# First expert stage of a four-layer attention and mixture-of-experts kernel: one region per expert over both turns, 71 tiles instead of 78, all its rows written inside the block before it

## The chip, the core and the metric

One Trainium2 chip, one core of it. The metric is device time in microseconds (us), the median of several executions. All times are from the profile of one execution, or from the timed runs where that is said. The engines are called PE (TensorE), DVE (VectorE), ACT (ScalarE), POOL or GpSimd, and SP (SyncE, which here only issues DMAs).

## The reference, cut to what matters

`x` is [32, 128, 128]: 4096 rows of 128 values. Four layers, each an attention and an expert stage, each added to x:

```python
x = x + _L0_xattn_ref(ctx_1024, _layernorm(x), ...)     # two hops of softmax attention over ctx
x = x + _L0_ffn_ref(_layernorm(x), router_w, w1, b1, w2, b2)
x = x + _L1_xattn_ref(_layernorm(x), ctx_1024, ...)     # linear attention, 16 heads of 8
x = x + _L1_ffn_ref(_layernorm(x), ...)                 # top 2 of 8, capacity 256 rows an expert
x = x + _L2_xattn_ref(ctx_1024, _layernorm(x), ...)     # 16 heads of 64 over ctx and x
x = x + _L2_ffn_ref(_layernorm(x), ...)                 # top 2 of 8, silu gate
x = x + _L3_xattn_ref(_layernorm(x), ctx_1024, ...)     # one head
x = x + _L3_ffn_ref(_layernorm(x), ...)                 # top 1 of 8
```

The first expert stage, which the change is named for, is, for each row,

```python
router_logits = x @ router_w.T
topk_values, topk_indices = top_k(router_logits, 2)      # of 8 experts
topk_weights = softmax(topk_values)
h1 = gelu(x @ w1[e].T + b1[e])                           # 128 -> 512
expert_outputs = h1 @ w2[e].T + b2[e]                    # 512 -> 128
mixed_output = sum over the two chosen e of topk_weights * expert_outputs
```

## The kernel before, in words

The kernel is a row of blocks. A block is one program for each engine; at its end every engine waits for all the others, GpSimd's queue ends with a drain, and then the next block begins. In order: a small load block, `attention_0`, `experts(0)`, `attention_1`, `route(1)`, `experts(1)`, `attention_2`, `experts(2)`, `attention_3`, `experts(3)` and the final sum and store. Below they are also called the first attention, the first expert stage, and so on.

**Attentions 0, 1 and 3** work in two turns (TURNS) of four interleaved streams (W) of four 128-row tiles (G), so 16 tiles (N) a turn. Each turn ends with a layer norm, the router logits, and the top two of them. In attention 0 the engines then count how many rows go to each expert (two matmuls with a triangle and with ones, L808), DVE copies the counts (`counted`, L896) and works out for every row its place in a table in DRAM (`places`, L902, which ends with `first_positions`). GpSimd then writes the rows there: `spread_row` (L657) is one indirect DMA of 128 rows of 129 words, of which the last word is the number of the output row. Each tile goes out twice, for the first and the second choice; between the two GpSimd rewrites the last word (`second_choice`, L664, which ends with a GpSimd drain). Both turns make 64 such DMAs. SP writes a tile of padding at the end of each expert's rows (L716 to L721), for each turn.

**The table of the first expert stage** (`xturn`) has a region for each expert and turn, each padded to whole tiles, so the stage has 2 x 39 = 78 tiles (TILES_FIRST) to work through. The order of the tiles and the expert of each come from `tile_tables` (L629), called once a turn at the end of attention 0. Because the regions are kept apart by turn, the stage can start when the first turn's rows are there: of the second turn's 32 DMAs, 8 are issued inside attention 0 (L764), 7 at the start of the stage (LAST_ROWS_AHEAD), and the other 17 one by one behind its scatters (`late_spread`, L670, and L1319).

**An expert stage** is a pipeline over tiles of 128 rows. SP loads the tile of rows into one of eight slots (`load_tile`, L1258); PE turns it; DVE copies the turned tile and the 516 columns of the expert's first weights (L1414, L1416); PE makes the hidden rows (L1345); ACT applies gelu (L1379); PE makes the output (L1357); DVE adds the bias (L1408) and GpSimd scatters the 128 output rows to their places in DRAM (L1318). SP's first loads are issued after the stage has begun, in stage 0 after it has waited for padding and rows. In stages 0 and 3 ACT issues a 512 KB load of the second bias (`load_b2`, L1252), and DVE waits for it before its first copy. Stages 2 and 3 are the same with 71 and 39 tiles; stage 2 has a silu gate and no bias. Stage 1 gathers its rows by another path.

**Weights.** Stage 1's weights (3 MB) are loaded by SP inside stage 0, behind the first eight tiles (L1272). Stage 3's (4 MB) are loaded by ACT, first thing in stage 2 (L1387).

**Attention 2** has 128 units (32 tiles by four quarters of the heads) in a software pipeline, so its head runs before the first unit can start: SP brings four tiles' pairs of expert rows (512 KB, `stage`, L1836); GpSimd multiplies and adds them into x (`add_pairs`, L1914), DVE takes mean and variance and makes the reciprocal root by a bit trick and three Newton steps (`seed`, `refine`, L2158 to L2167), GpSimd scales the rows (`scale_rows`), PE turns them and ACT keeps them. The context rows take a path of their own (`norm_context`). At the end of attentions 2 and 3 GpSimd waits until all spread rows have landed (L1993, L2394), and the block ends.

## Time and profile before

| | |
|---|---|
| median of 3 runs | 1893.69 us (1891.07 to 1894.52) |
| the profiled execution | 1896.3 us; its span 1894.4 us |
| busy in the span | PE 79%, weight loads 71%, DVE 62%, ACT 44%, POOL 41% |
| mean granted TensorE clock | 0.865 of full speed |
| DMA | 84.67 MB, mean 45 GB/s |

Stages on the profile's clock, read from SP's timeline (the first DMA that SP issues in a block comes less than 1 us after the block has begun): attention 0 to 199.6; expert stage 0 from there to 404.6; attention 1, route and stage 1 to 670.5; attention 2 to 1467.2; stage 2 to 1617.2; attention 3 to 1781.7; stage 3 to 1875.9; final sum to 1894.4.

How to read it: the busy shares are means over stages with different limits, and an engine that is idle in one stage says nothing of the next. The chain of waits that the profile prints reaches back only to the last block's start, so for a change in the earlier blocks the timelines at the block borders have to be read instead.

### The profile page before, as it was taken

What the parts mean: (1) busy time and instruction counts of PE and PEld (TensorE: products, weight loads), DVE (VectorE), ACT (ScalarE), POOL (GpSimd) and SP (SyncE); (2) the same over time, 40 slices, a digit from 0 to 9 for tenths busy, and PEclk for the clock granted to TensorE, in tenths of its full rate; (3) what the DMA queues carried; (4) which work ended last, traced back from release to release, by engine and by line L of the source; (5) the groups of instructions that cost most, each with busy time, mean ns of one, the idle gap of its engine ahead of it and who ended that gap; (6) DMA issues with size and microseconds to landing.
All of it is one profiled execution on the core that took longest, in us unless ns stands there. A gap on an engine that the chain in (4) does not pass through costs nothing. (4 is left out here: it accounts for less than half of the span.)

```text
span 1894.4 us, 37385 instructions
## 1 busy us (share of the span) xinstructions
PE 1492.4 (79%) x10501; PEld 1343.0 (71%) x10502; DVE 1165.8 (62%) x3709; ACT 834.1 (44%) x2565; POOL 776.9 (41%) x769
## 2 busy tenths in 40 slices
PE   6575589966577639999999999999993798446294
PEld 4454579954466639999999999999993787235294
DVE  4536234438867337787877777777775455575244
ACT  3342335531222226666666666666661232323152
POOL 2034454420000635454747575656454355012442
PEclk8776789987766769999999999999997899766697
DMA  9311422230011120000000000000001522200223
GB/s 231 13 29 41 136 58 64 64 107 0 1 45 45 41 93 13 1 12 1 24 1 22 1 21 11 11 3 8 4 10 35 149 72 66 90 7 16 64 65 115
DMA packets 96551, 84.67 MB, mean 45 GB/s; under 512 B 17444, under 2 KB 83207, under 8 KB 96327
## 3 DMA queue, kind: packets, MB, share of 16 engines
q1 hardware_dynamic: 75048, 49.50, 10.3%
q0 software_dynamic: 12160, 25.01, 3.9%
q10 hardware_dynamic: 9248, 9.05, 1.6%
q8 instruction: 41, 0.67, 0.1%
q14 instruction: 54, 0.44, 0.1%
HBM read 52.92 MB, written 32.70 MB: 45 GB/s over the span
## 5 line engine op out<-in xcount | busy, mean ns | idle before, releaser
L1973 POOL TENSOR_TENSOR paired_rows<-paired_rows,rinv 128x1024 f32<-128x1024 f32 x128 | 242.5, 1895 | 284.9 <-DVE rinv L2258 281.7
L2137 ACT ACTIVATE paired_rows<-psum_banks,neg_max 128x256 f32<-128x256 f32 x512 | 237.8, 490 | 0.2
L2249 DVE TENSOR_TENSOR probs_turned_lo<-psum_banks,probs_turned_hi 128x512 fp32r<-128x512 f32 x256 | 175.6, 686 | 97.6 <-ACT probs_turned_hi L2119 84.3
L2023 PE MATMUL psum_banks<-y_turned_parts,queries_hi 128*128 128x256 f32 x1024 | 200.7, 294 | 3.0 <-DVEq L1874 3.0
L2058 PE MATMUL psum_banks<-probs_turned_hi,y_rows 128*128 128x512 f32 x512 | 192.2, 416 | 0.4 <-issue 0.4
L2119 ACT CAST probs_turned_hi<-psum_banks 128x512 fp32r<-128x512 f32 x256 | 151.1, 590 | 57.2 <-PE psum_banks L2007 54.8
L2023 PEld LDWEIGHTS psum_banks<-y_turned_parts,queries_hi 128*128 128x128 f32 x1024 | 159.1, 192 | 3.5 <-issue 3.5
L2007 PE MATMUL psum_banks<-ident,paired_rows 128*128 128x128 f32 x1024 | 155.0, 274 | 7.4 <-DVEq L1874 4.4
L2263 DVE TENSOR_REDUCE neg_max<-psum_banks 128x4 f32<-128x1024 f32 x128 | 155.9, 1218 | 7.1 <-PE psum_banks L2023 3.5
L2119 ACT CAST queries_hi<-psum_banks 128x512 fp32r<-128x512 f32 x128 | 75.1, 587 | 172.0 <-PE psum_banks L2046 167.4
L2023 PE MATMUL psum_banks<-y_turned_parts,queries_lo 128*128 128x256 f32 x512 | 145.3, 284 | 0.0
L2070 PEld LDWEIGHTS psum_banks<-expert_w_a,paired_rows 128*128 128x128 f32 x1024 | 133.9, 191 | 11.8 <-DVE paired_rows L2273 1.0
L2046 PE MATMUL psum_banks<-expert_w_b,expert_w_a 128*128 (+1 forms) x1024 | 138.3, 278 | 3.3 <-ACT tail_turned L2109 1.8
L2070 PE MATMUL psum_banks<-expert_w_a,paired_rows 128*128 128x128 f32 x1024 | 134.9, 275 | 0.8 <-issue 0.8
L1379 ACT ACTIVATE hidden<-psum_banks,tile_w 128x128 f32<-128x128 f32 x312 | 89.6, 369 | 102.5 <-PE psum_banks L1345 77.1
L2046 PEld LDWEIGHTS psum_banks<-expert_w_b,expert_w_a 128*128 128x128 f32 x1024 | 125.8, 193 | 7.3 <-ACT tail_turned L2109 3.2
L2007 PEld LDWEIGHTS psum_banks<-ident,paired_rows 128*128 128x128 f32 x1024 | 119.5, 142 | 10.3 <-DVEq L1874 5.1
L2249 DVE TENSOR_TENSOR queries_lo<-psum_banks,queries_hi 128x512 fp32r<-128x512 f32 x128 | 88.4, 691 | 43.1 <-ACT queries_hi L2119 34.6
L2137 ACT ACTIVATION_READ_ACCUMULATOR paired_rows<-psum_banks,neg_max 128x1 f32 x512 | 113.2, 221 | 0.0
L1318 POOL DMA_INDIRECT expert_rows<-expert_rows_sb,tile_rows x78 | 76.8, 985 | 80.7 <-DVE expert_rows_sb L1408 77.1
L2058 PEld LDWEIGHTS psum_banks<-probs_turned_hi,y_rows 128*128 128x128 f32 x512 | 96.3, 188 | 17.7 <-issue 0.5
L658 POOL DMA_INDIRECT rows_by_expert_and_turn<-paired_rows,top_experts x64 | 62.0, 969 | 111.5 <-ACT u_turned___ L841 60.6
(699 smaller groups left out, 3440.5 us busy)
## 6 DMA issues: line engine op xcount, KB each, us to landing
paired_rows<-expert_rows SPq DMA_DIRECT2D x16, 512.0 KB, 6.0
tile_rows<-rows_by_expert_and_turn SPq DMA_DIRECT2D x78, 64.5 KB
tile_rows__<-rows_by_expert SPq DMA_DIRECT2D x71, 64.5 KB
staged_pairs<-expert_rows SPq DMA_DIRECT2D x8, 512.0 KB
tile_rows___<-rows_by_expert SPq DMA_DIRECT2D x39, 64.5 KB
x_rows<-in_x_dram SPq DMA_DIRECT2D x8, 256.0 KB, 5.4
expert_w_b<-in_L_ffn_w_dram SPq DMA_DIRECT2D x1, 2048.0 KB
normed_rows_dram<-paired_rows SPq DMA_DIRECT2D x1, 2048.0 KB, 8.8
```

Of the source, the lines that this page charges most:

```text
L1318: pool.indirect_dma_start(ys, bass.IndirectOffsetOnAxis(ap=to, axis=0), yo[:, i % SLOTS, :], None).then_inc(expert_out[i % SLOTS].sem, 16)
L1379: ins = act.activation(hidT[:, s % 2, c * P:(c + 1) * P], hidden_bank(s, c // 2)[:, c % 2 * P:(c % 2 + 1) * P], ACT.Gelu, bias=w1[:, s % 4 ...
L1973: ins = pool.tensor_tensor(probs[:, p, :, :], probs[:, p, :, :], rinv[:, p, :].unsqueeze(2).to_broadcast([P, 4, 256]), ALU.mult)
L2007: ins = pe.transpose(bank[T_BANK][:, h * P:(h + 1) * P], probs[:, par, h, c * P:(c + 1) * P], ident[:, :])
L2023: ins = pe.matmul(bank[S_BANKS[par] + h // 2][:, (h % 2) * 256:(h % 2 + 1) * 256], queries[q][:, h, :], yparts[:, 2 * s2 + y, :], start=(k ...
L2046: ins = pe.matmul(bank[Q_BANK][:, h * P:(h + 1) * P], wqk[:, 4 * u3 + h, :], flat(KVT[:, bass.ds(b3, 1), P:2 * P]), start=True, stop=True)
L2058: ins = pe.matmul(bank[Z_BANK][:, :], yrows[:, 2 * s1 + y, k * P:(k + 1) * P], probsT[p][:, (u + 1) % 2, k, :], start=(k == 0 and n == 0), ...
L2070: ins = pe.matmul(bank[Y_BANK][:, 0:P], mixed[:, par, h, :], wvo[:, 4 * u0 + h, :], start=(u0 == 0 and h == 0), stop=(u0 == 3 and h == 3), ...
L2119: ins = act.copy(dst, bank[bank_][:, :])
L2137: ins = act.activation(probs[:, par, h, :], bank[S_BANKS[par] + h // 2][:, (h % 2) * 256:(h % 2 + 1) * 256], ACT.Exp, bias=nmax[:, par, h: ...
L2249: ins = dve.tensor_tensor(lo, bank[bank_][:, :], hi.bitcast(F32), ALU.subtract)
L2263: ins = dve.tensor_reduce(nmax[:, par, :], ps[:, S_BANKS[par]:S_BANKS[par] + 2, :].rearrange("p r (h k) -> p (r h) k", k=256), AX.X, ALU.m ...
```

## The change

The table `xfirst` takes the place of `xturn`: one region per expert over both turns, so the first expert stage has 71 tiles. The second turn's counts begin where the first's ended (`begin` from `ends0`), `tile_tables` is called once, and padding is written once (8 DMAs instead of 16). All 64 row DMAs are issued inside attention 0. `second_choice` no longer drains GpSimd; it waits on a semaphore of its own copy. At the end of attention 0 SP waits for all rows and loads the first two tiles (AHEAD) of the next stage before the block ends; attentions 2 and 3 do the same, and there GpSimd's wait for the rows moves to SP. The slots for tiles (`tile_rows`) are therefore one buffer for the whole kernel. Stage 1's weights are loaded in attention 1, stage 3's in attention 3, both by SP behind the pairs. In attention 0 PE waits for DVE's copy of the counts only before stream 0's keys in the next turn, and ACT's small exponential comes after the weight copies. In attention 2's head DVE does the first four tiles' sums, ACT makes the roots by logarithm and exponential, and DVE scales the rows; GpSimd only scales the context rows. Parts of the diff that rename or move buffers are left out below.

```diff
-TILES_TURN = (B * P + E * (P - 1)) // P
-TILES_FIRST = 2 * TILES_TURN
-TURN_TILES = E * TURN_REGION // P + E - 1
...
-            for i in range(TURNS):
-                at = (i * TURN_TILES + E * TURN_REGION // P) * P
-                mine = 2 * E + i * SPARE_TILES
-                sp.dma_start(as_tiles(xturn[at:at + SPARE_TILES * P, :]), pad_tiles[:, mine:mine + SPARE_TILES, :]).then_inc(pads_stored.sem, 16)
+            sp.dma_start(as_tiles(xfirst[E * REGION:, :]), pad_tiles[:, 2 * E:2 * E + SPARE_TILES, :]).then_inc(pads_stored.sem, 16)
...
+        def rows_are_here(sp):
+            for c in first_rows_spread:
+                sp.wait_ge(c.sem, TURNS * 16 * N)
+
+        def place_first_pads(sp):
+            sp.wait_ge(first_ends.sem, 1)
+            for e in range(E):
+                at_ = sp.value_load(first_pad_at[0:1, e:e + 1], min_val=0, max_val=E * REGION - P)
+                sp.dma_start(xfirst[bass.ds(at_, P), :], pads_dram[e * P:(e + 1) * P, :]).then_inc(first_pads.sem, 16)
+
+        def load_rows(sp, layer, j, s, free):
+            rows = xfirst if layer == 0 else xb
+            at = sp.value_load(tile_base[0:1, bass.ds(j, 1)], min_val=0, max_val=E * REGION // P + SPARE_TILES - 1)
+            if not isinstance(j, int) or j >= SLOTS:
+                free()
+            src = rows.rearrange("(t p) d -> t p d", p=P)[bass.ds(at, 1), :, :].rearrange("a p d -> (a p) d")
+            sp.dma_start(tile_rows[:, s, :], src).then_inc(tile_loaded[s].sem, 16)
+
+        def load_first_tiles(sp, layer):
+            sp.wait_ge(tables_made.sem, tables_made.value + 1)
+            for j in range(AHEAD):
+                load_rows(sp, layer, j, j, None)
...
-            pool.tensor_copy(ROWS.bitcast(U32)[:, at, P], odd_number[:, at])
-            pool.drain()
-
-        def late_spread(pool):
-
-            for t in range(N // 2, N):
-                spread_row(pool, TURNS - 1, 0, t)
-                yield
-            for half in range(2):
-                second_choice(pool, TURNS - 1, half)
-                for t in range(half * N // 2, (half + 1) * N // 2):
-                    spread_row(pool, TURNS - 1, 1, t)
-                    yield
...
-                    for i in range(TURNS):
-                        sp.wait_ge(first_ends.sem, i + 1)
-                        for e in range(E):
-                            at_ = sp.value_load(first_pad_at[0:1, i * E + e:i * E + e + 1], min_val=0, max_val=2 * TURN_TILES * P - P)
-                            n = (i * E + e) * P
-                            sp.dma_start(xturn[bass.ds(at_, P), :], pads_dram[n:n + P, :]).then_inc(first_pads.sem, 16)
+                    place_first_pads(sp)
+                    sp.wait_ge(first_pads.sem, 16 * E)
+                    rows_are_here(sp)
+                    load_first_tiles(sp, 0)
...
-                    spread_first(pool, 1, 0, 0)
+                    for half in range(2):
+                        spread_first(pool, 1, 0, half)
+                    for half in range(2):
+                        second_choice(pool, 1, half)
+                        spread_first(pool, 1, 1, half)
...
+                        if w == 0:
+                            pe.wait_ge(first_places_read.sem, i + 1)
...
-                        dve.tensor_copy(begin[:, 0, :], region[:, i, :])
+                        dve.tensor_copy(begin[:, 0, :], ends0[:, i - 1, :] if i else region[:, :])
...
-                    def turn_is_here(i):
-                        for c in first_rows_spread:
-                            sp.wait_ge(c.sem, (i + 1) * 16 * N)
-                    if layer == 0:
-                        sp.wait_ge(first_pads.sem, 16 * TURNS * E)
-                        turn_is_here(0)
+                        load_rows(sp, layer, j, s, lambda: slot_is_free(sp, j, s))
                     if kept:
-                        for j in range(SLOTS):
+                        for j in range(AHEAD, SLOTS):
                             load_tile(j, j)
-                    if layer == 0:
-                        load_expert_weights(sp, layer + 1)
...
-                        loops = [(1, n_tiles // SLOTS)]
-                        if layer == 0:
-                            loops = [(1, TILES_TURN // SLOTS), (TILES_TURN // SLOTS + 1, n_tiles // SLOTS)]
-                        for turn, (begin_, end_) in enumerate(loops):
-                            if turn:
-                                for j in range(loops[0][1] * SLOTS, begin_ * SLOTS):
-                                    if j == TILES_TURN:
-                                        turn_is_here(1)
-                                    load_tile(j, j % SLOTS)
-                            with sp.Fori(begin_, end_) as q:
-                                for u in range(SLOTS):
-                                    load_tile(q * SLOTS + u, u)
+                        with sp.Fori(1, n_tiles // SLOTS) as q:
+                            for u in range(SLOTS):
+                                load_tile(q * SLOTS + u, u)
...
-                    late = late_spread(pool) if layer == 0 else iter(())
-                    for _ in range(LAST_ROWS_AHEAD):
-                        next(late, None)
...
-                    if layer == 2:
-                        load_expert_weights(act, layer + 1)
...
                     load_pairs(sp, layer_before)
+                    load_expert_weights(sp, 1)
...
                     place_pads(sp, range(E // 2), 0)
                     sp.wait_ge(pads_placed.sem, 16 * E)
+                    sp.wait_ge(rows_spread.sem, 16 * 2 * G * NG)
+                    load_first_tiles(sp, 2)
...
-                    for c in range(10):
-                        norm_part(0, c)
+                    norm_context(0)
...
+                def roots(act, own, which):
+                    act.wait_ge(spread_known.sem, spread_known.value + which)
+                    act.activation(row_work[:, 2, own], row_work[:, 0, own], ACT.Ln, scale=-2.0)
+                    act.drain()
+                    act.activation(row_rstd[:, own], row_work[:, 2, own], ACT.Exp, scale=-0.5).then_inc(roots_made.sem, 1)
...
-                    dve.wait_ge(pairs_combined.sem, 1)
+                    dve.wait_ge(pairs_staged.sem, 16)
+                    for k in range(2):
+                        for j in range(G):
+                            xt = x_tile(0)(j)
+                            ins = dve.scalar_tensor_tensor(xt, staged[:, j, k, :], WT[:, k, j:j + 1], xt, ALU.mult, ALU.add)
+                        ch.link()
+                    dve.sem_inc(pairs_combined.sem, 1)
                     row_stats(dve, ch, 0, 0)
                     aggregate(dve, ch, [0])
-                    seed(dve, ch)
-                    refine(dve, ch, 3)
-                    keep_scales(dve, ch, 0, None)
+                    dve.tensor_scalar(row_work[:, 0, :], row_mv[:, :, 1], -0.5 * (1.0 + EPS), -0.5 * EPS * EPS, ALU.mult, ALU.add).then_inc(spread_known.sem, 1)
+                    dve.wait_ge(roots_made.sem, roots_made.value + 1)
+                    refine(dve, ch, 1)
+                    for j in range(G):
+                        ins = dve.tensor_scalar(latents[:, j, :], x_tile(0)(j), row_mv[:, j, 0:1], row_rstd[:, j:j + 1], ALU.subtract, ALU.mult)
+                    ins.then_inc(latents_normed.sem, 1)
+                    dve.sem_inc(scales_made.sem, 1)
                     all_steps(lambda eng, i, c: dve_step(eng, ch, i, c))(dve)
...
                     load_pairs(sp, layer_before)
+                    load_expert_weights(sp, 3)
                     place_pads(sp, range(E // 2), 1)
                     sp.wait_ge(pads_placed.sem, 2 * 16 * E)
+                    sp.wait_ge(rows_spread.sem, 16 * (2 * B + B))
+                    load_first_tiles(sp, 3)
 
```

## Rows read from the trace of the kernel before

**Rows 1.** Stretches of the first and last expert stages; columns in the first line.

```profile
core 0: us, PE busy (x) PEld busy (x) DVE busy (x) ACT busy (x) POOL busy (x), PEclk, DMA share, GB/s
...
212.00:224.00 12.00, 8.91 (x74) 8.26 (x72) 4.04 (x13) 4.94 (x18) 4.58 (x7) 1.00 0.94 299
...
224.00:271.00 47.00, 32.87 (x213) 31.20 (x213) 11.12 (x36) 14.10 (x49) 28.01 (x30) 0.82 0.24 63
...
271.00:387.00 116.00, 115.55 (x937) 109.82 (x938) 53.10 (x166) 63.29 (x223) 54.61 (x56) 0.99 0.21 62
...
1792.00:1870.00 78.00, 76.73 (x632) 72.40 (x630) 35.36 (x110) 42.32 (x148) 37.86 (x39) 1.00 0.20 58
```

**Rows 2.** GpSimd in the first attention: start us, us, instruction, idle before and releaser.

```profile
145.26 0.21 POOL L667 COPY paired_rows<-odd_number 128x8 uint32<-128x8 uint32 x1
...
148.01 0.98 POOL L658 DMA_INDIRECT rows_by_expert_and_turn<-paired_rows,top_experts  x1 [2.55 <-issue]
...
182.65 0.96 POOL L658 DMA_INDIRECT rows_by_expert_and_turn<-paired_rows,top_experts  x1 [12.52 <-DVE top_experts L913]
...
200.34 0.96 POOL L658 DMA_INDIRECT rows_by_expert_and_turn<-paired_rows,top_experts  x1 [7.59 <-POOLq L682]
```

**Rows 3.** GpSimd in the first expert stage, same columns.

```profile
211.24 0.96 POOL L1318 DMA_INDIRECT expert_rows<-expert_rows_sb,tile_rows  x1 [2.36 <-DVE expert_rows_sb L1408]
...
274.07 0.96 POOL L1318 DMA_INDIRECT expert_rows<-expert_rows_sb,tile_rows  x1 [1.77 <-DVE expert_rows_sb L1408]
...
395.55 0.96 POOL L1318 DMA_INDIRECT expert_rows<-expert_rows_sb,tile_rows  x1 [0.30 <-DVE expert_rows_sb L1408]
```

**Rows 4.** GpSimd's queue, drains that end four blocks, by source line; ns min/median/max.

```profile
L682 POOLq DRAIN  x1: 9023/9023/9023, 185.8 to 185.8; - x1
...
L1781 POOLq DRAIN  x1: 1354/1354/1354, 1465.8 to 1465.8; - x1
...
L2352 POOLq DRAIN  x1: 2656/2656/2656, 1778.8 to 1778.8; - x1
...
L1196 POOLq DRAIN  x1: 5845/5845/5845, 1611.2 to 1611.2; - x1
```

**Rows 5.** Timelines: first and last expert stage begin (ACT, SP), last stage's scatters (GpSimd).

```profile
200.47 11.49 SPq L1264 DMA_DIRECT2D tile_rows<-rows_by_expert_and_turn  x8
...
1781.76 0.36 ACTq L1252 DMA_DIRECT2D expert_b___<-in_L_ffn_b_dram  x1
...
1792.20 0.98 POOL L1318 DMA_INDIRECT expert_rows<-expert_rows_sb___,tile_rows___  x1 [14.87 <-DVE expert_rows_sb___ L1408]
...
1869.87 0.97 POOL L1318 DMA_INDIRECT expert_rows<-expert_rows_sb___,tile_rows___  x1 [0.31 <-DVE expert_rows_sb___ L1408]
```

**Rows 6.** Timelines (GpSimd, DVE): head of the third attention; priced DVE work of other heads.

```profile
674.43 0.18 POOL L1916 COPY group_scale<-mix_weights 128x4 f32<-128x4 f32 x1 [8.50 <-DMA staged_pairs<-expert_rows]
...
687.24 1.04 POOL L1928 TENSOR_TENSOR latents_normed<-latents_normed,group_scale 128x512 f32<-128x512 f32 x1
...
429.57 2.34 DVE L524 SCALAR_TENSOR_TENSOR x_rows<-paired_rows,mix_weights,x_rows 128x128 f32<-128x128 f32 x8
...
1440.92 0.87 DVE L2149 BATCH_NORM_STATS2 rows_stats<-x_rows 128x6 f32<-128x128 f32 x4
...
1443.77 2.14 DVE L2331 TENSOR_SCALAR paired_rows<-x_rows,rows_mv,rows_rstd 128x128 f32<-128x128 f32 x8
```

**Rows 7.** Timelines where the third and fourth expert stages begin (GpSimd, SP, PE).

```profile
1463.16 0.97 POOL L1963 DMA_INDIRECT rows_by_expert<-paired_rows,top_experts  x1 [0.30 <-issue]
...
1468.08 23.33 SPq L1264 DMA_DIRECT2D tile_rows__<-rows_by_expert  x12
...
1475.56 0.45 PE L1335 MATMUL psum_banks<-ident,tile_rows__ 128*128 128x128 f32 x1 [24.11 <-DMA tile_rows__<-rows_by_expert]
...
1785.70 0.66 PE L1335 MATMUL psum_banks<-ident,tile_rows___ 128*128 128x128 f32 x2 [32.63 <-DMA tile_rows___<-rows_by_expert]
```

**Rows 8.** PE timeline where the first attention's second turn begins; same columns as rows 2.

```profile
90.83 2.39 PE L621 MATMUL psum_banks<-ident,expert_w_a 128*128 128x128 f32 x10 [1.18 <-DVE places L899]
```

More of the change, by code:

```diff
@@ L37 @@
 REGION = B * P + P
[L38 removed]
 SLOTS = 8
+AHEAD = 2
 RSQRT_SEED = 1597463007.0
@@ L1196, in experts @@
             with ExitStack() as ph:
-                xr = sb_in(ph, "tile_rows", [P, SLOTS, P + 1 if kept else P])
+                xr = tile_rows
                 xt = sb_in(ph, "tile_turned", [P, 2, P])
```

98 lines of the change are left out of this document (46 added, 52 removed).

## The prediction

> **What bounds the kernel now.** Every stage has its own limit, so I read the windows of the expert stages first, then the timelines of GpSimd, DVE, SP and PE at each block border. In full flow an expert stage is bound by PE: 76.73 of 78 us busy over the last stage's 39 tiles, and 115.55 of 116 us in the later part of stage 0, at a granted clock of 1.00 and 0.99 [rows 1]. The last stage's pace is (1869.87 − 1792.20) / 38 = 2.044 us a tile [rows 5]. The first third of stage 0 is not like that: PE is busy 32.87 of 47 us in 224 to 271, GpSimd 28.01 us with 30 instructions, the clock 0.82, and in 212 to 224 the DMA engines are 0.94 busy with the 3 MB of weights [rows 1]. Tile 0 is scattered at 211.24 and tile 18 at 274.07: 3.49 us a tile. From there to tile 77 at 395.55 it is 121.48 / 59 = 2.06 [rows 3]. GpSimd is the one that holds the early tiles: a row DMA takes 0.96 us with 0.30 between two [rows 2, 3], so a late row DMA and a scatter together take 2.53 us a tile, and two drains come on top. The attentions' insides are hardly touched by the change; what counts there is each head and each end.
>
> **Stage 0's start: +29.7 us.** Before, the block ends at 199.6, because of PE and ACT turning the next weights; GpSimd's drain had ended at 185.8 + 9.02 = 194.8 [rows 4]. Its eight row DMAs of turn 2 began at 182.65 after a wait for DVE [rows 2], so they ended at 182.65 + 8 x 1.26 = 192.7, and the drain took 2.0 us more, for 16 DMAs. After, 32 row DMAs follow, and they outlast all else. PE no longer waits 1.18 us for DVE at the turn's border [rows 8], so I start them at 181.45. 32 x 1.26 is 40.4. Two `second_choice` copies come among them; a copy is 0.21 us [rows 2], with its wait I take 0.5 each. Bounds: nothing, or 2.55 each as the gap after a drained one had [rows 2]; I take the low side since the drain is what goes. With 0.3 for a hiccup the last DMA ends at 223.2. The 48 DMAs that such drains had shared now wait for the block's end: drains cost 1.354, 2.656 and 5.845 us after 16, 32 and 71 indirect DMAs [rows 4], 0.082 each; for 16 in attention 0 it was 2.0, so 0.7 is fixed there, and 64 give 0.7 + 5.3 = 6.0. SP meanwhile waits for the rows to land (1.6 us after the last one's end: 1463.16 + 0.97 [rows 7] to the drain of L1781 at 1465.8 [rows 4]) and issues two tile loads at 11.49 / 8 = 1.44 each [rows 5]: 4.5 us, under the drain. If the drain were free, the block would end only 1.5 us sooner. The stage starts at 223.2 + 6.0 + 0.1 = 229.3 instead of 199.6.
>
> **Stage 0 itself: −42.9.** I take the last stage for its pattern, as it has no late rows and no weight load beside it. From the b2 load at 1781.76 to the first scatter at 1792.20 are 10.4 us [rows 5]; stage 0 had 211.24 − 199.6 = 11.6, which is −1.2. The 18 slow steps at 2.044 take 36.8 instead of 62.8: −26.0. The 59 at 2.06 lose 0.9 (they still hold some late rows and drains). Seven tiles fewer: −14.3. The end's drain follows 71 scatters and not 77: −0.5. The last scatter is then at 229.3 + 10.4 + 70 x 2.044 = 382.8 against 395.55, −12.8, and with the drain **−13.2** for attention 0 and stage 0 together. The tile loads before the block's end earn little: b2 is waited for in any case, as the last stage's first copy is, and it is issued where it was. One padding set and one table fewer lie beside PE's weights and cost nothing either way; bound 0 to −1.
>
> **Weights moved: 0.** Stage 1's 3 MB now go behind the pairs in attention 1, whose first use is DVE's at 429.57 [rows 6]. Stage 0's own load ran at 299 GB/s [rows 1], so 3.15 MB take 10.5 us; if the pairs shared all of that they could come up to 10.5 us later. The 4 MB behind attention 3's pairs take 14 us at the same rate. I take zero since SP issues the pairs first and the weights' issue comes behind them; the upper bounds go into the range. The Trainium skill, page "DMA: Bandwidth & Descriptors", section "Issuing engines are not separate DMA queues", says that transfers of all issuers run on the same 16 engines and interleave. By that alone the pairs would share with the weights and the whole sum would be near −3; no row here shows pairs beside weights.
>
> **Attention 2's head: −7.5.** Before: GpSimd begins at 674.43 when the pairs are there and its last scaling ends at 687.24 + 1.04 = 688.28 [rows 6]: 13.85 us. After, DVE: eight multiply-adds, 2.34 us in attention 1; then in attention 3, where the root is already made by ACT with one refinement, from the statistics at 1440.92 to the first scaling at 1443.77 are 2.85 us, for four tiles; then four scalings at 2.14 / 8, 1.07 [rows 6]. With 0.1 between, 6.36. The 0.3 to 1 us that the last step may cost more is in the range. GpSimd stood idle 8.50 us before 674.43 [rows 6], and `norm_context` needs no pairs, so its work, about two operations like the one of 1.04, is over by then. The Trainium skill, "SBUF — State Buffer" (the single rule on the shared port pair), says that a DVE instruction with two SBUF inputs and a GpSimd instruction that reads SBUF block each other. DVE's multiply-adds are such; by that page a late `norm_context` would put up to 2.1 us on the head, making −5.4. The idle row speaks against their meeting.
>
> **Stage 2's start: −6.4.** The block starts at 1467.2 and PE gets its tile at 1475.56 [rows 7], beside the 4 MB that ACT loads. After, SP waits until the rows are in (1465.8 [rows 4]) and issues two loads, so the block starts 0.9 later, at 1468.1; a tile is there, and PE turns it about 1.1 us after the start, 1469.2. The pace behind it is PE's, so the gain is kept. **Stage 3's start: −0.8.** GpSimd's drain of 2.656 us [rows 4] no longer stands behind the landing but beside SP's loads, 0.3; the b2 load is alone, 0.5 of the 3.9 between its issue at 1781.76 and PE's work at 1785.70 [rows 5, 7]. Bounds 0 and −2.
>
> **Sum.** −13.2 − 7.5 − 6.4 − 0.8 = −27.9, from the profiled execution's 1896.3 to 1868.4. That execution lies 2.6 above the median of 1893.69, so on the median I say **1866**. 0.2%, 3.8 us, is about what a measurement can tell from no change.
>
> **Rivals.**
> - *The end of attention 0 costs more*: `second_choice` keeps its gap of 2.55 and the drain grows faster than 0.082 a DMA: +7, 1873. For: the long drains there. Chance 0.10.
> - *The early loads hide nothing*, the wait moving ahead of the block's end, and stages 2 and 3 win zero: +7, 1873. For: SP's waits are on GpSimd's last DMA, which is on the path. Against: PE's 8.4 us at 1475.56. Chance 0.08.
> - *Weights beside pairs*: less than half of the bounds of 10.5 + 14 comes through, +10 (at most 24.5), 1876. Chance 0.06.
> - *More is won*: stalls in attention 0 of several us that no row ties to work vanish with the shorter programs, or the early tiles run at stage 0's own best: −7, 1859. Chance 0.10.
> - *The early tiles stay slow* for another reason than the late rows, their slots or the clock: the 26.0 stay, 1892, no difference. Against: 28.01 us of GpSimd in 47. Chance 0.03.
> - *Slower: PE's clock does not come back.* PE now stands idle some 30 us at the end of attention 0. A tile holds 76.73 / 39 = 1.97 us of PE at clock 1.00 [rows 1], so at the lower level (1.2 of 2.4 GHz) it costs 2.0 more; from 14 tiles on (27.9 / 2.0) the change loses, with all 71 it is 1866 + 140 = 2006. Against: the last stage begins after 32.63 us of PE idleness [rows 7] and shows clock 1.00 from 1792 [rows 1]. Chance 0.02.
>
> The forecast keeps 0.60; 0.01 is for what I don't see. Its own spread is ±5 from the bounds on `second_choice`, drain, b2 and DVE's head. The range of 1856 to 1881 adds the rivals at 1859, 1873 and most of 1876. Faster by over 0.2%: 0.60 + 0.10 + 0.08 + 0.06 + 0.10 = 0.94; same 0.03; slower 0.03.
>
> **What would show it.** The last row DMA of attention 0 ends near 223 and its drain takes 5 to 6 us; stage 0's b2 load is issued at 229 to 230; 71 scatters, the first near 240, the last near 383, evenly 2.04 apart and never two GpSimd DMAs to a tile. In attention 1, DVE's first multiply-add on pairs keeps its distance from the block's start. In attention 2, pairs landed to first scaled tile is about 6.4 us. In stage 2, PE's first turn comes within 1.5 us of the block's start. I am wrong if the block-end drain is over 10 us, if early steps stay over 2.5 us, if pairs land late, or if a low clock lasts beyond stage 0's tenth tile.

## The result, and the profile after

| | before | after |
|---|---|---|
| median | 1893.43 us (1891.07 to 1894.52, 5 runs) | 1876.02 us |
| the others | | 1871.54, 1872.86, 1882.34 |
| profiled execution | 1896.3 us | 1872.9 us, span 1871.1 |

The ratio is 0.9907, with an interval of 0.9884 to 0.9930: faster by 17.4 us by the medians and by 23.4 us between the two profiled executions, where 27.9 were forecast. A fifth run of the changed kernel took 3680 us, which the median of 1876.02 counts (without it, it is 1874.4), the ratio leaves out, and no profile shows. Block by block, each from one GpSimd signal at the block's end to the next (the last column is from two profiles of the experiments below, r5_before and r1_again, which ran on two other chips):

| block | before | after | difference | forecast | difference on the other chips |
|---|---|---|---|---|---|
| attention 0 | 194.6 | 233.3 | +38.7 | +29.7 | 174.8 to 209.4, +34.6 |
| stage 0 | 205.1 | 162.8 | −42.3 | −42.9 | 192.1 to 162.6, −29.5 |
| attention 1 | 186.6 | 180.9 | −5.7 | 0 | 187.8 to 185.3, −2.5 |
| route, stage 1 | 79.3 | 77.4 | −1.9 | 0 | 72.4 to 71.1, −1.2 |
| attention 2 | 796.8 | 790.4 | −6.4 | −6.6 | 795.5 to 788.7, −6.8 |
| stage 2 | 149.9 | 141.8 | −8.1 | −7.3 | 130.8 to 123.5, −7.3 |
| attention 3 | 164.5 | 165.5 | +1.0 | −0.3 | 158.5 to 157.6, −0.9 |
| stage 3, final | 112.7 | 113.9 | +1.2 | −0.5 | 113.9 to 113.2, −0.7 |

Stage 0 as a whole came out as computed here. Windows of the changed kernel:

```profile
core 0: us, PE busy (x) PEld busy (x) DVE busy (x) ACT busy (x) POOL busy (x), PEclk, DMA share, GB/s
200.00:230.00 30.00, 0.27 (x1) 0.14 (x1) 0.73 (x3) 3.60 (x9) 23.03 (x26) 0.53 0.18 56
230.00:250.00 20.00, 7.01 (x33) 6.49 (x34) 2.18 (x7) 3.78 (x9) 2.27 (x3) 0.51 0.22 63
250.00:271.00 21.00, 20.89 (x177) 19.93 (x175) 9.63 (x30) 11.66 (x41) 9.99 (x11) 1.00 0.21 59
271.00:387.00 116.00, 115.95 (x966) 111.51 (x965) 53.99 (x171) 64.73 (x228) 57.06 (x57) 1.00 0.22 63
```

From 250 us on, when the first tile is scattered, PE is busy almost without a gap at a granted clock of 1.00, where the first third had 32.87 of 47 us at 0.82 [rows 1]. The price stands in the first line: 30 us with PE doing nothing. GpSimd's timeline of the same stretch, against [rows 2, 3]:

```profile
191.78 0.96 POOL L678 DMA_INDIRECT rows_by_expert_first<-paired_rows,top_experts  x1 [30.89 <-DVE top_experts L927]
...
231.92 0.95 POOL L678 DMA_INDIRECT rows_by_expert_first<-paired_rows,top_experts  x1 [0.30 <-issue]
250.27 0.95 POOL L1306 DMA_INDIRECT expert_rows<-expert_rows_sb,tile_rows  x1 [17.40 <-DVE expert_rows_sb L1393]
...
392.52 0.96 POOL L1306 DMA_INDIRECT expert_rows<-expert_rows_sb,tile_rows  x1 [0.30 <-DVE expert_rows_sb L1393]
```

First scatter to last are (392.52 − 250.27) / 70 = 2.03 us a tile. The first one comes 12.0 us after the block's start (238.3), where it was 11.7 before and 10.4 were forecast. From the second turn's first row DMA to the end of the last are 232.87 − 191.78 = 41.1 us, and the block's end follows at 238.3; its drain had been queued at 222.8, while the last DMAs still ran:

```profile
L691 POOLq DRAIN  x1: 15339/15339/15339, 222.8 to 222.8; - x1
```

222.8 + 15.34 is 238.2, so the drain ends 5.3 us after the last DMA (232.87). What is wrong against the forecast is the beginning: GpSimd gets the second turn's places from DVE at 191.78 and not at 181.45. DVE's timeline shows where the time is:

```profile
137.78 0.18 DVE L893 RECIPROCAL rinv___<-sums___ 128x4 f32<-128x4 f32 x1 [1.22 <-issue]
153.09 1.13 DVE L901 SCALAR_TENSOR_TENSOR x_rows<-psum_banks,rinv,x_plus_u 128x128 f32<-128x128 f32 x4 [15.12 <-remote]
162.94 1.13 DVE L901 SCALAR_TENSOR_TENSOR x_rows<-psum_banks,rinv_,x_plus_u_ 128x128 f32<-128x128 f32 x4 [8.73 <-remote]
```

And PE's of the same time:

```profile
138.95 1.16 PE L809 MATMUL psum_banks<-ctx_rows,expert_w_a 128*128 x8 [0.48 <-ACT expert_w_a L862]
141.01 1.16 PE L809 MATMUL psum_banks<-ctx_rows,expert_w_a 128*128 x8 [0.91 <-issue]
143.88 4.19 PE L809 MATMUL psum_banks<-ctx_rows,expert_w_a 128*128 x16 [1.70 <-ACT expert_w_a L862]
174.22 1.11 PE L577 MATMUL psum_banks<-ident,u_rows 128*128 128x128 f32 x4 [26.15 <-DVE u_rows L475]
```

DVE is free at 138. PE shows stream 0's second mixing at 138.95 (the first 8 of 32 matmuls) and nothing after the last of them until 174, but the first result reaches DVE only at 153.09 and the next at 162.94: waits of 15.1 and 8.7 us. "remote" means that the trace holds no instruction that released DVE. No edit touches the mixing.

The head of attention 2, and PE at the starts of stages 2 and 3, against [rows 6, 7]:

```profile
663.12 2.35 DVE L2308 SCALAR_TENSOR_TENSOR x_rows<-tile_rows,mix_weights,x_rows 128x128 f32<-128x128 f32 x8 [3.10 <-DMA tile_rows<-expert_rows]
665.59 0.87 DVE L2140 BATCH_NORM_STATS2 rows_stats<-x_rows 128x6 f32<-128x128 f32 x4
...
668.46 1.11 DVE L2317 TENSOR_SCALAR latents_normed<-x_rows,rows_mv,rows_rstd 128x128 f32<-128x128 f32 x4
```

```profile
1450.11 0.45 PE L1322 MATMUL psum_banks<-ident,tile_rows 128*128 128x128 f32 x1 [17.49 <-PEq L1767]
1450.96 0.48 PE L1322 MATMUL psum_banks<-ident,tile_rows 128*128 128x128 f32 x1 [0.41 <-DMA tile_rows<-rows_by_expert]
...
1757.37 0.45 PE L1322 MATMUL psum_banks<-ident,tile_rows 128*128 128x128 f32 x1 [28.43 <-PEq L2352]
...
1762.52 1.83 PE L1332 MATMUL psum_banks<-tile_turned___,tile_w___ 128*128 128x128 f32 x7 [3.66 <-DVE tile_w___ L1401]
```

Pairs to the last scaled row of tile group 0: 669.57 − 663.12 = 6.45 us, where it was 13.85; 6.36 were forecast. Stage 2's first tile is turned 0.3 us after the block's start instead of 8.3. In stage 3 the tile is there at once as well, but PE's first real matmul comes at 1762.52, 5.3 us after the b2 load is issued at 1757.19; before it was 5.2.

### The profile page after: what moved, and what is told of

It reads as the page before. It is cut to its first block and busy times, and to the rows that moved or that the text cites. A ratio compares the mean times of both kernels' runs of the same rounds, so it can differ in the third digit from the quotient of the medians.

```text
span 1871.1 us, 36757 instructions
## 1 busy us (share of the span) xinstructions
PE 1460.7 (78%) x10382; PEld 1312.4 (70%) x10383; DVE 1155.9 (62%) x3674; ACT 826.0 (44%) x2538; POOL 763.2 (41%) x753
## 5 line engine op out<-in xcount | busy, mean ns | idle before, releaser
L1961 POOL TENSOR_TENSOR paired_rows<-paired_rows,rinv 128x1024 f32<-128x1024 f32 x128 | 242.3, 1893 | 286.0 <-DVE rinv L2249 282.9
L1322 PE MATMUL psum_banks<-ident,tile_rows 128*128 128x128 f32 x197 | 56.9, 289 | 91.8 <-PEq L691 36.8
L1366 ACT ACTIVATE hidden<-psum_banks,tile_w 128x128 f32<-128x128 f32 x284 | 81.2, 368 | 69.1 <-PE psum_banks L1332 69.1
L678 POOL DMA_INDIRECT rows_by_expert_first<-paired_rows,top_experts x64 | 62.2, 972 | 112.2 <-ACT u_turned___ L854 62.6
```

What stands on the lines that cost most here:

```text
L678: pool.indirect_dma_start(xfirst, bass.IndirectOffsetOnAxis(ap=first_spots[:, i, k, t:t + 1], axis=0), ROWS[:, i * N + t, :], None).then_i ...
L1366: ins = act.activation(hidT[:, s % 2, c * P:(c + 1) * P], hidden_bank(s, c // 2)[:, c % 2 * P:(c % 2 + 1) * P], ACT.Gelu, bias=w1[:, s % 4 ...
L1961: ins = pool.tensor_tensor(probs[:, p, :, :], probs[:, p, :, :], rinv[:, p, :].unsqueeze(2).to_broadcast([P, 4, 256]), ALU.mult)
```

## The experiments

The twelve kernels ran on three chips, four on each (r1 to r4, r5 to r8, r9 to r12). The kernel before has medians of 1828.1, 1828.0 and 1827.6 us there, 65 us under the first table's, so these times compare with each other and not with the first table. The record does not number the chip of the first table; I call it the first chip, though the same chip in another condition isn't ruled out. One caution for all: attention 1, whose instructions the edits hardly touch, took 180.3 to 189.9 us in these profiles, and the ten times of the changed kernel in r1_again lie in two groups, 1813.8 to 1818.3 and 1822.1 to 1823.9. Medians are therefore good to 3 or 4 us here, and I read each edit in the block it belongs to.

**Does the late result repeat, and is it GpSimd's stream of DMAs?** After the first profile my theory S was that the stream without the drain's gaps holds the other engines up. Four kernels: the changed one again; the drain back in `second_choice`; the kernel before with the semaphore in its first turn alone; and the changed one with 24 row DMAs held until PE has made the mixing.

```diff
 # r2_drain_back
-            pool.tensor_copy(..., odd_number[:, at]).then_inc(second_choices.sem, 1)
-            pool.wait_ge(second_choices.sem, 2 * i + half + 1)
+            pool.tensor_copy(..., odd_number[:, at])
+            pool.drain()
 # r3_sem_before, against the kernel before
-            pool.drain()
+            if i == 0: the copy counts, pool.wait_ge(second_choices.sem, half + 1)
+            else: pool.drain()
 # r4_after_mixing
                     weave(body(w, TURNS - 1, SS[w], T[w], False) for w in range(W))
+                    for w in range(W):
+                        pool.wait_ge(SS[w].pe.sem, SS[w].PE.at(TURNS - 1, "mixed1"))
                     spread_first(pool, 0, 0, 1)
```

> The changed kernel once more, to see what repeats. In its first profile TensorE's results of the second mixing in the first attention's second turn came to DVE at 153.09 and 162.94 us, 15.1 and 8.7 us after DVE was free, while GpSimd issued row DMAs one behind another; the second turn's rows were ready at 191.8 instead of the 181.4 that I had forecast. Theory S (the gapless stream of indirect DMAs holds the other engines up): the stalls are there again, 15 to 30 us in sum, and the gate at 188 to 196. Rival N (chance of one execution): the gate lies at 170 to 182 here and the total near 1862 to 1866. Total by S: 1871 to 1882.

> The changed kernel with the drain back in second_choice, in both turns. Theory S (the stream without gaps is what stalls): the stream is cut after 8 DMAs as in the kernel before, stalls in the second turn shrink to 10 us or less, the gate comes back to 181 to 184, which is -9; two drains in the second turn cost 2 x 2.3 more and the drain at the block's end falls from 5.5 to 3, so the total is 5 to 9 us under the changed kernel. Rival F (the stalls come from something else, such as the place of the code or a late fetch of instructions): the gate stays at 188 to 196 and the total is 1 to 3 us above.

> The kernel before with one edit: second_choice of the first turn waits on a semaphore of its copy instead of draining. Theory S: the gaps of 2.55 and 2.23 us in the stream vanish, and PE's results of the second mixing come later; the second turn's first row DMA moves from 182.65 to 188 to 195 and the total rises by 5 to 12 us. Rival F: the first row DMA of the second turn stays at 180 to 184 and the total is the same within 2 us, as GpSimd is idle there before the second turn's rows anyway.

> The changed kernel, with 24 of the first turn's 32 row DMAs held until TensorE has made the second mixing of the second turn. Theory S: DVE gets the second mixing at about 141 instead of 153 to 163; the stream of 24 then runs from 143 to 174 beside layer norm and router, where it may cost 3 to 6 us as in the kernel before; the gate comes to 172 to 180 and the total falls by 10 to 18 us to 1858 to 1866. Rival F: the stall stays where it is in the code (153 and 163), the held DMAs end at 195 and push the end of the block, total 0 to 10 us above the changed kernel.

| | median | ratio to before (interval) | second turn's first row DMA | attention 0 |
|---|---|---|---|---|
| r1_again | 1817.61 | 0.9940 (0.9919 to 0.9960) | 167.90 | 209.4 |
| r2_drain_back | 1820.56 | 0.9962 (0.9946 to 0.9978) | 168.06 | 212.7 |
| r3_sem_before | 1831.21 | 1.0013 (0.9996 to 1.0029) | 166.19 | 174.8 |
| r4_after_mixing | 1817.99 | 0.9953 (0.9935 to 0.9972) | 171.59 | 212.2 |

All of S's numbers missed. In r1_again the stream of DMAs is just as gapless, and DVE waits 2.70 us and then nothing:

```profile
134.57 0.18 DVE L893 RECIPROCAL rinv___<-sums___ 128x4 f32<-128x4 f32 x1 [1.22 <-ACT probs___ L858]
137.46 1.13 DVE L901 SCALAR_TENSOR_TENSOR x_rows<-psum_banks,rinv,x_plus_u 128x128 f32<-128x128 f32 x4 [2.70 <-PE psum_banks L809]
138.50 1.12 DVE L901 SCALAR_TENSOR_TENSOR x_rows<-psum_banks,rinv_,x_plus_u_ 128x128 f32<-128x128 f32 x4
```

The drains put back bring no earlier gate and lengthen attention 0 by 3.3 us (their gaps of 2.90 and 2.22 us in the second turn instead of 0.28 each, less a shorter drain at the end). The semaphore in the kernel before changes nothing clear of noise. Holding the rows back only delays them. So S is dead: the stream alone does not make the results late. The first chip has such waits in both kernels, all put down to "remote": in the kernel before 6.6 us at 123.16 in attention 0, 7.8 and 5.8 in stage 0, 5.2 in stage 1 and 11.5 in attention 3; in the changed one also 5.2 in stage 1 and 14.3 in attention 3. The other chips are not quite free of it. Eight of the twelve profiles have one "remote" wait of 4.2 to 5.6 us at 64 to 67 us, as here in r1_again, and in none do PE, DVE or ACT have another over 1.5 us:

```profile
66.15 1.12 DVE L901 SCALAR_TENSOR_TENSOR x_rows<-psum_banks,rinv_,x_plus_u_ 128x128 f32<-128x128 f32 x4 [5.37 <-remote]
```

Late loading of code is a rival, and for the two long waits the trace speaks against it: between 120 and 170 us of the changed kernel's first profile there is no transfer of instructions, only GpSimd's row DMAs. None of this could be tried on the first chip again, and the cause stays open.

**The kernel before on these chips.**

> The kernel before, for a profile on the chip of the experiments, where it takes 1828 instead of 1893 us. Theory C (on the first chip TensorE's results came late in several places, here they do not): the second turn's first row DMA at 164 to 168 us and not at 182.65; attention 0 about 173 to 176 us long; stage 0 about 190 instead of 205, with fewer waits of DVE on late results. Rival (the second chip is faster in all): attention 0 and stage 0 shorter in the same ratio as the rest, 3 to 4%, so 188 and 198.

This kernel ran once, 1832.9 us. The gate (the second turn's first row DMA) is at 167.65, attention 0 takes 174.8 and stage 0 192.1 us, as C said; DVE has none of the "remote" waits in stage 0. GpSimd:

```profile
167.65 0.96 POOL L658 DMA_INDIRECT rows_by_expert_and_turn<-paired_rows,top_experts  x1 [6.35 <-DVE top_experts L913]
...
192.18 0.95 POOL L1318 DMA_INDIRECT expert_rows<-expert_rows_sb,tile_rows  x1 [2.97 <-DVE expert_rows_sb L1408]
...
246.28 0.96 POOL L1318 DMA_INDIRECT expert_rows<-expert_rows_sb,tile_rows  x1 [0.31 <-issue]
```

Two of my sizes hang on this. The block ends at 179.9, 12.2 us after the gate; on the first chip it was 16.9, with ACT waiting 4.5 and 3.8 us for late results. And tile 0 to tile 18 take 54.1 us, 3.0 a tile, not 62.8. With the changed kernel's gate at 167.90 and its block's end at 214.4, 46.5 us later just as on the first chip, attention 0 and stage 0 together come to +34.6 − 29.5 = +5.1 us here, and that already counts what two side edits save in the two blocks (the semaphore for the drains, and the weights moved out of stage 0). The named part loses; the next run shows how much.

**The first-stage part undone, all the rest kept.** Regions by turn, 78 tiles and late rows again; this kernel has everything else of the change, and its late `second_choice` uses the semaphore too.

```diff
 # r6_rest_only, against the changed kernel
-            n_tiles = {0: TILES_TOP2, ...
+            n_tiles = {0: TILES_FIRST, ...
-                    for half in range(2):
-                        spread_first(pool, 1, 0, half)
-                    for half in range(2):
-                        second_choice(pool, 1, half)
-                        spread_first(pool, 1, 1, half)
+                    spread_first(pool, 1, 0, 0)
...
+                    late = late_spread(pool) if layer == 0 else iter(())
```

> The changed kernel with its first-stage part undone: regions by turn, 78 tiles, late rows beside the scatters, no rows waited for at the end of attention 0. Kept are attention 2's head, the early tile loads and the moved waits of attentions 2 and 3, both weight moves, the turn border and second_choice's semaphore. Theory L (on this chip the first-stage part loses: attention 0 grows by 35 us, stage 0 shrinks by 28): this kernel is 7 to 14 us faster than the changed one, 1803 to 1811, since stage 0 here also loses the weight load beside it and a drain. Rival G (the part gains the 13 us that I forecast, or any): this kernel is 3 to 13 us slower than the changed one, 1821 to 1831.

1808.38 us, ratio 0.9888 (0.9866 to 0.9911, against 0.9919 to 0.9960 for r1_again): 9.2 under the changed kernel's median and 19.6 under the kernel before, so it beats both. Attention 0 and stage 0 take 173.8 + 184.9 = 358.7 us, against 372.0 in the changed kernel and 366.9 before. So with the side edits in place the named part costs 13.3 us in its two blocks, and the side edits alone save 8.2 there. Theory L holds.

**What makes the early tiles slow?** Two kernels put one thing back each.

```diff
 # r10_rest_late_drain, against r6_rest_only
-            pool.wait_ge(second_choices.sem, 2 * i + half + 1)
+            if i == 1: pool.drain()
+            else: pool.wait_ge(second_choices.sem, 2 * i + half + 1)
 # r11_rest_weights1, against r6_rest_only
-                    load_expert_weights(sp, 1)          # in attention 1
+                    if layer == 0:
+                        load_expert_weights(sp, layer + 1)   # in stage 0
```

> The kernel with the first-stage part undone, and in stage 0 the two late second_choice calls drain GpSimd again. Theory Q (stage 0's slow early tiles are GpSimd's queue: a late row DMA and a scatter to each tile, and two drains): the gaps of 6.6 and 2.7 us come back, stage 0 takes 192 to 194 instead of 184.9 us, the total is 6 to 9 us above 1808. Rival B (PE or the slots bind there and the drains are covered): stage 0 within 2 us of 184.9.

> The kernel with the first-stage part undone, and stage 1's 3 MB back in stage 0 behind the first eight tiles. Theory Q (GpSimd's queue binds, the weights are beside it): stage 0 within 2 us of 184.9, attention 1 unchanged. Rival D (the weights' 10 us of the DMA engines hold tiles and late rows up): stage 0 longer by 3 to 8 us.

GpSimd in r6_rest_only, r10_rest_late_drain and r11_rest_weights1 (tile 0's scatter, the copy in `second_choice` and what follows it, tile 18's scatter):

```profile
190.75 0.96 POOL L1332 DMA_INDIRECT expert_rows<-expert_rows_sb,tile_rows  x1 [2.67 <-DVE expert_rows_sb L1420]
...
194.48 0.21 POOL L684 COPY paired_rows<-odd_number 128x8 uint32<-128x8 uint32 x1
194.97 0.98 POOL L675 DMA_INDIRECT rows_by_expert_and_turn<-paired_rows,top_experts  x1 [0.28 <-POOL paired_rows L684]
...
236.32 0.96 POOL L1332 DMA_INDIRECT expert_rows<-expert_rows_sb,tile_rows  x1 [0.30 <-issue]
```

```profile
187.37 0.96 POOL L1335 DMA_INDIRECT expert_rows<-expert_rows_sb,tile_rows  x1 [1.99 <-DVE expert_rows_sb L1423]
...
191.10 0.20 POOL L684 COPY paired_rows<-odd_number 128x8 uint32<-128x8 uint32 x1
194.62 0.97 POOL L675 DMA_INDIRECT rows_by_expert_and_turn<-paired_rows,top_experts  x1 [3.32 <-issue]
...
238.01 0.96 POOL L1335 DMA_INDIRECT expert_rows<-expert_rows_sb,tile_rows  x1 [0.30 <-issue]
```

```profile
187.78 0.96 POOL L1334 DMA_INDIRECT expert_rows<-expert_rows_sb,tile_rows  x1 [2.50 <-DVE expert_rows_sb L1422]
...
234.50 0.96 POOL L1334 DMA_INDIRECT expert_rows<-expert_rows_sb,tile_rows  x1 [0.30 <-issue]
```

Without drains tile 0 to 18 take 45.57 us, 2.53 a tile, which is within 0.01 of two DMAs of 0.96 with 0.30 behind each (2.52); GpSimd's timeline has no gap over 0.35 us in that stretch. With the drains it is 2.81, with the weights 2.60. So the queue of GpSimd is the bound. But the drains cost the stage only 2.8 us (187.7 against 184.9), not the 7 to 9 that I expected. Their gaps here are 3.32 and 2.47 us where the kernel before had 6.6 and 2.7, so tile 18 is only 5.1 us later, and 2.1 of that come back: without them all DMAs are counted in the drain at the stage's end, which takes 8.38 us in r6_rest_only and 6.25 in r10_rest_late_drain. The weights alone cost 1.2 (186.1). Both together, as in the kernel before, cost tile 18 54.1 − 45.6 = 8.5 us, more than the 5.1 and 1.2 apart; the first drain's gap is 6.6 us with the weights beside it and 3.3 without. The medians are 1810.18 (0.9904; 0.9883 to 0.9926) and **1802.15** (0.9869; 0.9848 to 0.9890). The latter is the fastest kernel of the study; it is 8 us under r10 on the same chip, but 3.0 of it is attention 1 (183.9 against 186.8), which I can't tell from that block's own spread, so whether the weights are better left in stage 0 is not settled.

**The drain at the block's end.** One more drain between the turns' rows, where GpSimd is idle.

```diff
 # r9_mid_drain, against the changed kernel
+                    pool.drain()
                     kept_and_placed(pool, SS, 1)
```

> The changed kernel with one more GpSimd drain in attention 0, between the two turns' rows, where GpSimd stands idle 10 us. My forecast's term for the block's end (a drain costs 0.082 us for each indirect DMA since the last one): the drain at the end falls from 5.4 to about 2.6 us and SP's two tile loads decide the end; last row DMA to the block's end 4.5 instead of 5.4 us, the total 1 us less, which only the trace can show. Rival (the drain's length is not set by the count): 5.4 us as before.

The end's drain in r1_again and in r9_mid_drain:

```profile
L691 POOLq DRAIN  x1: 15342/15342/15342, 199.0 to 199.0; - x1
```

```profile
L691 POOLq DRAIN  x1: 12732/12732/12732, 198.4 to 198.4; - x1
```

It ends 5.3 us after the last DMA in the first and 2.7 in the second: 2.6 us for 32 DMAs fewer, 0.082 each. SP's two loads then decide the block's end, which comes 3.98 us after the last DMA instead of 5.43. The median, 1820.44 of 7 runs (0.9953; 0.9929 to 0.9977), can't show these 1.4 us.

**Attention 2's head.** The old head in the changed kernel.

```diff
 # r7_old_head
-                    norm_context(0)
+                    for c in range(10):
+                        norm_part(0, c)
...
+                    dve.wait_ge(pairs_combined.sem, 1)
                     row_stats(dve, ch, 0, 0)
                     aggregate(dve, ch, [0])
+                    seed(dve, ch)
+                    refine(dve, ch, 3)
+                    keep_scales(dve, ch, 0, None)
```

> The changed kernel with attention 2's head as before (GpSimd adds and scales, DVE makes roots by bit trick and three steps). My forecast for this term was 7.5 us: 1825, attention 2 at 796 us instead of 788.7. Rival (the head is hidden by something else, the context's path or the weights): attention 2 stays within 2 us of 788.7.

GpSimd, from the pairs' arrival to the last scaling:

```profile
633.82 0.18 POOL L1904 COPY group_scale<-mix_weights 128x4 f32<-128x4 f32 x1 [8.00 <-DMA tile_rows<-expert_rows]
...
646.63 1.04 POOL L1916 TENSOR_TENSOR latents_normed<-latents_normed,group_scale 128x512 f32<-128x512 f32 x1
```

13.85 us again, attention 2 at 796.0 instead of 788.7, the median 1827.80 (0.9995; 0.9979 to 1.0012). The term is 7.3 us. With it taken out, the changed kernel is no faster than the one before here.

**Stage 2: the early tile or the moved weights?**

```diff
 # r8_weights3_act: load_expert_weights(sp, 3) out of attention 3, and in stage 2
+                    if layer == 2:
+                        load_expert_weights(act, layer + 1)
 # r12_no_early_tiles: load_first_tiles(sp, 2) and (sp, 3) out, and
-                        for j in range(AHEAD, SLOTS):
+                        for j in range(AHEAD if layer == 0 else 0, SLOTS):
```

> The changed kernel with stage 3's 4 MB back in stage 2, issued by ACT. Theory W (the tile came late in stage 2 because it shared the DMA engines with the weights; the early load cures that by itself): stage 2's first transposition still comes within 1.5 us of the block's start, but tiles 2 to 7 are loaded beside the weights and come late: stage 2 longer by 2 to 6 us, attention 3 unchanged. Rival E (the early load alone brings the gain): stage 2 at 123.5 us as in the changed kernel, within 1 us. Rival D (the move costs in attention 3): attention 3 is 3 us or more shorter than 157.6.

> The changed kernel, with stages 2 and 3 loading all their tiles inside the stage again; SP still waits for the rows in the attentions, the weights stay moved. Theory W (in stage 2 the weights beside the tiles cost the most, 6.4 of the 7.4 us won, as the run with the weights back on ACT has shown, and the early load about 1): stage 2 126 to 127 instead of 123.5, attention 2 two tile loads shorter (-2), so the total is the same within 2 us. Rival E (the early load is worth 3 us or more by itself): the total is 3 to 5 us above the changed kernel.

PE in r8_weights3_act, its window and the same window of r1_again, and PE in r12_no_early_tiles:

```profile
1418.39 0.45 PE L1322 MATMUL psum_banks<-ident,tile_rows 128*128 128x128 f32 x1 [17.32 <-DMA tile_rows<-rows_by_expert]
...
1426.10 0.48 PE L1322 MATMUL psum_banks<-ident,tile_rows 128*128 128x128 f32 x1 [4.38 <-DMA tile_rows<-rows_by_expert]
```

```profile
core 0: us, PE busy (x) PEld busy (x) DVE busy (x) ACT busy (x) POOL busy (x), PEclk, DMA share, GB/s
1418.00:1433.00 15.00, 9.84 (x54) 9.05 (x55) 4.74 (x14) 3.29 (x8) 1.40 (x2) 0.59 0.96 287
```

```profile
1422.00:1437.00 15.00, 14.19 (x101) 13.60 (x102) 8.65 (x26) 5.29 (x15) 4.84 (x5) 0.81 0.23 60
```

```profile
1419.96 0.44 PE L1322 MATMUL psum_banks<-ident,tile_rows 128*128 128x128 f32 x1 [17.62 <-DMA tile_rows<-rows_by_expert]
```

With the weights back (287 GB/s) the first tile is early, 0.3 us after the start, and the third then comes 4.38 us late; stage 2 takes 129.9 us, 6.4 more than 123.5, and attention 3 is not shorter without them (157.8 against 157.6). Without the early loads, PE's first tile comes 2.8 us after the block's start (1417.19); stage 2 takes 125.6, 2.1 more, and attention 2 ends 1.6 sooner. The medians are 1822.94 (0.9987; 0.9969 to 1.0005) and 1814.40 (0.9929; 0.9910 to 0.9948). The moved weights are the gain (in the eight profiles on these chips with weights moved and early tiles kept, stage 2 takes 123.4 to 124.3 us); the early tiles by themselves are worth nothing that these runs can tell.

## Why the prediction was right or wrong

The direction and the range held: 1876 lies between 1856 and 1881. The size did not: 17.4 us instead of 27.9. Between the profiled executions 4.4 us are missing: attention 0 paid 9.0 us more than forecast, and attention 1 gave 5.7 that were not in the forecast. The other 6.0 are the distances of these two executions from their medians (2.9 above before, 3.2 below after). The direction is owed to the side edits. The term that the change is named for, −13.2 for attention 0 and stage 0, came out at 38.7 − 42.3 = −3.6 on the first chip and at +5.1 on the others, and taken by itself it costs 13.3 us in its blocks (r6_rest_only). That the change still won by 0.6% there and 0.9% on the first chip is luck in so far as the main term had the wrong sign.

**The step that failed is "I start them at 181.45".** The other parts of that term held: 41.1 us for the 32 row DMAs and two copies (41.7 forecast; `second_choice` costs 0.5 as taken, not 2.55), 5.3 for the drain (6.0; 64 x 0.082 is 5.2, so the fixed 0.7 was not there). But the start was read from one execution in which PE's results came late, and I took the time as work. On the first chip the changed kernel met later results (191.78); on the other chips, without the long waits, the gate stands at 167.65 before and 167.90 after (so the 1.2 us taken off for PE's wait did not show either), and the block before ends 12.2 us behind it, not 16.9. The cost of the new ending is then 34.3 us from gate to end, not 29.7.

**"The 18 slow steps … −26.0" was right in its cause and too large for a chip without the long late results.** GpSimd's two DMAs a tile are the floor at 2.53, as worked out from the row; the rest of the 3.49 was drains and weights (0.47 together, 8.5 us by 18) and, on the first chip, another 0.49, for which the late results are the likely but untested cause. There the stage gave back 42.3 against 42.9. Elsewhere it gives 29.5, against 34.6 paid. The −1.2 before the first scatter did not come (12.0 us against 11.7); DVE's first copy, which waits for b2, comes 4.7 us after b2's issue, where it came 4.8 after it. So the rival in which the first-stage part loses existed, and I had not priced it: my slower case was the clock, which came back with the first tiles (0.51 in 230 to 250, 1.00 from 250 on), and the rival about `second_choice` and the drain had the right place for the wrong reason.

**Weights moved: 0, right.** DVE's first sum on pairs in attention 1 stands 22.8 us after the block's start, before it was 24.9, although the 3 MB were on their way (246 GB/s in the first 30 us). Over all fourteen profiles it is 22.4 to 25.8 us with the weights there and 22.7 to 25.8 without, so they don't move it. What the block as a whole pays is not settled: r11_rest_weights1, without them, is 3.0 us shorter there than r10_rest_late_drain. In attention 3 r8_weights3_act takes the 4 MB away, and the block is 0.1 us longer, so they cost nothing that shows. By the Trainium skill's page "DMA: Bandwidth & Descriptors", section "Issuing engines are not separate DMA queues", transfers that different engines issue run on the same 16 DMA engines. The runs agree where it counts: in stage 2 tiles and weights are issued side by side, and PE waits 4.38 us for the third tile. In the attentions the pairs are issued first and needed late, and no such wait shows.

**Attention 2's head: −7.5, right** (−7.3 by r7_old_head). GpSimd's context work ended at 662.11, 1.0 us before DVE's first sum at 663.12, so the rule that the forecast took from the Trainium skill's page "SBUF — State Buffer" has no case here in which DVE and GpSimd meet.

**Stage 2's start: −6.4 by the sum, and −6.4 is what the weights alone bring.** The number was right, its cause half: I had PE's late tile cured by loading it early. Loading it early only moves the wait to the third tile. **Stage 3: −0.8 did not come on the first chip.** Attention 3 and stage 3 with the end took 2.2 us more there and 1.6 less on the others, which the blocks' own spread covers. b2 is waited for as before (5.3 us from its issue to PE's first real matmul, before 5.2), so what I called the bound of 0 is nearer.

**Not in the forecast:** −5.7 in attention 1 is inside that block's own spread of 180.3 to 189.9 us. Without it the profiled execution would stand at 1878.6.

## What to carry to other kernels

When a stage must wait for a producer that one queue serves, price the cover that is lost: here 24 row DMAs that had run beside matmuls at 1.26 us each became 30 us of an idle PE, and seven tiles fewer did not pay for them. Before a start time is read from a trace, look whether the waits ahead of it end on work or on nothing visible; the latter are no part of the work and may not be there in the next execution. And of a change with several parts undo each by itself: without the part that gave the change its name the kernel was 9 us faster by the medians, while with either of two side edits undone, a head moved from GpSimd to DVE and 4 MB of weights issued where nothing waits for a tile, no gain clear of noise was left (0.9995 and 0.9987).

## What the runs showed of the hardware

The same kernel took 1893 us in the first runs and 1828 on three chips of the experiments. Part of it is in plain sight: in the first runs DVE and ACT waited up to 15 us for results of PE after the dispatch that the trace shows, with "remote" as the releaser, in attentions 0 and 3 and stage 1 of both kernels and in stage 0 of the kernel before. Part of it I have not followed up: stage 2 took 149.9 against 130.8 us at a granted clock of 1.00 in the middle of both, with DVE idle for 15.6 of 100 us before its copies of turned tiles and nothing that the trace names as the reason.

At the end of an expert stage a GpSimd drain lasts 0.082 us for each indirect DMA since the last drain: 5.84 us for 71, 6.25 for 76, 8.38 for 102. Queued right behind row DMAs it ends 1.7 us after the last of 8, 2.0 to 2.3 of 16, 2.4 of 24, 2.7 of 32, 3.3 of 40 and 5.3 of 64, so the same rate holds from 32 on and a short drain costs more than its count. In stage 0, where scatters and row DMAs alternate, it ended 2.8 us after the last of 10 in r10_rest_late_drain and 6.1 in r5_before with the weights' load beside it. It is paid once: an early drain in an idle stretch took the first 32 DMAs off the block's end (r9_mid_drain).

Attention 1, hardly touched by any edit, differs by up to 9.6 us between profiles on one chip (180.3 in r2_drain_back, 189.9 in r4_after_mixing), which hides a smaller edit in a single profile's total.
